# Another order of expert products around layer 1's projections, and the first row maxima transposed in the ring before the attention

## What is computed

```python
def reference(x, ...):
    x = x + _L0_conv_ref(_gn(x), ...)          # 6 heads of 16, bias from rel_pos_h and rel_pos_w
    t = _to_tokens(x)
    t = t + _L1_attn_ref(_ln_t(t), ...)        # causal, 6 heads of 16
    t = t + _L1_ffn_ref(_ln_t(t), ...)         # all experts computed, weighted by masked gates
    return _from_tokens(t, x)
def _L1_ffn_ref(x, ...):
    h = jax.nn.gelu(jnp.einsum('bsd,edh->ebsh', x, w1) + b1[:, None, None, :], approximate=False)
    y = jnp.einsum('ebsh,ehd->ebsd', h, w2) + b2[:, None, None, :]
    return jnp.einsum('bse,ebsd->bsd', masked, y)
```

## Time and profile before

| | us |
|---|---|
| median of 3 runs | 2209.66 |
| lowest and highest run | 2201.82 to 2210.24 |
| the profiled execution | 2204.84 |
| its span, first to last instruction | 2203.0 |
| PE busy | 1855.9 (84%) |
| DVE busy | 1255.3 (57%) |
| ACT busy | 1121.6 (51%) |
| mean granted TensorE clock | 0.933 of full speed |

### The profile page before, as it was taken

One profiled execution on the slowest core, in us unless ns is written; L12 is line 12 of the kernel. 1 busy time (PEld: TensorE's weight loads), 2 busy tenths in 40 slices (PEclk: granted clock), 3 DMA queues, 4 the chain that ended last, 5 costly groups with the idle time before them and its releaser, 6 DMA issues.

```text
span 2203.0 us, 28891 instructions
## 1 busy us (share of the span) xinstructions
PE 1855.9 (84%) x9314; PEld 743.8 (34%) x9408; DVE 1255.3 (57%) x2512; ACT 1121.6 (51%) x1423; POOL 141.7 (6%) x68
## 2 busy tenths in 40 slices
PE   0279568998899988998889988999889988999848
PEld 0123223343333432343333433344323433334324
DVE  5384367736665566736675466645676456744611
ACT  0326434675456734566446734567346744555423
POOL 0000000200020000200011000200002000200020
PEclk9669769999999999999999999999899999999979
DMA  1702530263004430163002530063202530002100
GB/s 44 134 10 53 91 72 21 50 97 65 21 18 92 57 77 11 47 110 65 22 18 56 89 80 11 18 115 64 42 22 49 96 65 13 18 10 54 28 10 7
DMA packets 55741, 111.43 MB, mean 51 GB/s; under 512 B 17687, under 2 KB 18904, under 8 KB 54041
## 3 DMA queue, kind: packets, MB, share of 16 engines
q1 hardware_dynamic: 54040, 109.06, 26.3%
q10 hardware_dynamic: 1536, 0.30, 0.1%
HBM read 61.82 MB, written 34.60 MB: 44 GB/s over the span
## 4 chain that ended last, share of the span: by engine, by line
PE 67%; DVE 18%; issue 4%; ACT 4%; DMA 4%; SPq 1%; POOL 0%; DVEq 0%; POOLq 0%; ACTq 0%
PE psOM L629 15%; PE psS L574 12%; PE psT L607 8%; PE psT L606 7%; PE psT L741 6%; DVE mx L1236 6%; PE psS L755 4%; PE psT L609 3%; PE psT L536 3%; DVE mrow L1338 2%; DVE x L1347 2%; DVE qb L1365 1%; DMA qr<-negb 1%; PE psOM L561 1%; PE psT L545 1%
## 5 line engine op out<-in xcount | busy, mean ns | idle before, releaser
L968 ACT ACTIVATE probs<-psT 128x1024 f32<-128x1024 f32 (+7 forms) x768 | 622.6, 837 | 535.2 <-PE psT L607 265.9
L1236 DVE TENSOR_REDUCE mx<-psS 128x1 f32<-128x512 f32 (+3 forms) x1152 | 704.2, 643 | 305.2 <-PE psS L574 225.1
L607 PE MATMUL psT<-qb,kb 97*128 97x512 f32 x768 | 416.1, 586 | 6.9 <-DMA qb<-negr 5.9
L629 PE MATMUL psOM<-probs,v 128*32 128x512 f32 (+3 forms) x2688 | 386.2, 560 | 22.6 <-ACT probs L968 12.0
L574 PE MATMUL psS<-ka,qa 128*128 128x512 bf16 x722 | 283.4, 401 | 22.1 <-DVE mx L1236 14.0
L606 PE MATMUL psT<-qa,ka 128*128 128x512 bf16 x720 | 278.2, 386 | 11.4 <-DVE resid L1225 4.0
L741 PE MATMUL psT<-xf,w1s 97*128 97x512 f32 x384 | 193.8, 633 | 4.2 <-ACT probs L1025 2.4
L1365 DVE TENSOR_TENSOR qb<-psOM,qa 32x768 fp32r<-32x768 f32 x128 | 121.8, 952 | 127.7 <-ACT qa L1008 126.0
L609 PE MATMUL psT<-qr,kr 97*128 97x512 bf16 (+3 forms) x576 | 185.6, 349 | 5.3 <-DMA qr<-negb 1.6
L755 PE MATMUL psS<-probs,w2s 128*96 128x512 f32 x384 | 187.9, 612 | 0.0
L574 PEld LDWEIGHTS psS<-ka,qa 128*128 128x128 bf16 x768 | 71.6, 98 | 301.3 <-DVE mx L1236 265.1
(11 more groups left out here) (143 smaller groups left out, 1598.8 us busy)
## 6 DMA issues: line engine op xcount, KB each, us to landing
scr<-split SPq DMA_DIRECT2D x32, 576.0 KB, 4.3
scr<-qb SPq DMA_DIRECT2D x16, 768.0 KB, 6.7
qr<-scr SPq DMA_DIRECT2D x48, 192.0 KB, 6.8
au<-ot SPq DMA_DIRECT2D x192, 32.0 KB, 2.0
lb<-ot SPq DMA_DIRECT2D x192, 32.0 KB, 2.0
qr<-scr SPq DMA_DIRECT2D x48, 128.0 KB, 4.3
kr<-scr SPq DMA_DIRECT2D x48, 128.0 KB, 7.3
qa<-scr SPq DMA_DIRECT2D x32, 128.0 KB, 3.8
```

Source lines behind the costliest of these rows:

```text
L607: last = mm(o[:, a:b], kb[:, h, ks], qb[:, h, a:b], start=False, stop=True)
L629: last = mm(psO[j:j + 2 * HD, a - c * HALF:HALF], v[:, kt, 2 * p + hh, :], probs[:, (2 * kt + hh) % 4, a:(c + 1) * HALF], start=kt == 0, s ...
L968: A(probs[:, n % 4, q0:T], psT[:, t_slot(ts, m), q0:T], ACT.Exp).then_inc(t_free, 1)
L1236: V.reduce_max(mx[layer][:, p % 2, (h % 2) * NT + t, kc:kc + 1], psS[:, s_bank(st, fill), 0:max_cols(layer, t, kc)], AX).then_inc(s_free, 1)
```

## The change

The list MIX is reordered between `u3` and `m0`, `lev` goes ahead of `V0`, `u10` ahead of `b1`, and a step `tmax` is added at its end. `tmax` transposes the first maxima into a slot of psT instead of psM (`first_rows`), and ACT negates them and issues the DMA there (`first_negated`). `attention(it, 1)` no longer begins with the transposition, and the wait for the additions goes to the first value product. The counts of the semaphores follow. The number of instructions is the same but for the loop's waits.

```diff
-MIX = seq("gate gates u0 u1 R0 d0 H0 L0 H1 L1 v0 u2 d1 v1 ln den R1 u3 H2 L2 d2 H3 u4 res d3 nrm L3 u5 d4 tr u6 R2 H4 L4 d5 q0 q1 V0 lev V1 "
-          "H5 L5 u7 d6 u8 R3 H6 L6 d7 H7 L7 u9 b0 d8 b1 u10 m0 m1 m2 m3 d9 m4 m5 m6 "
-          "u11 m7 m8 m9 m10 d10 m11 m12 b2 m13 m14 d11 m15 b3")
+MIX = seq("gate gates u0 u1 R0 d0 H0 L0 H1 L1 v0 u2 d1 v1 ln den R1 u3 d2 u4 H2 L2 u5 res H3 d3 nrm L3 u6 d4 d5 tr R2 H4 L4 q0 q1 lev V0 d6 V1 "
+          "u7 H5 L5 R3 u8 d7 H6 L6 H7 L7 u9 b0 d8 u10 b1 m0 m1 m2 m3 d9 m4 m5 m6 "
+          "u11 m7 m8 m9 m10 d10 m11 m12 b2 m13 m14 d11 m15 b3 tmax")
...
             def transpose_max(it, layer, p):
                 ms, n = att_m(layer, p)
-                if layer == 1 and p == 0:
-                    pe.wait_ge(t_free, upto("t_free", it, ms, 0))
-                else:
-                    pe.wait_ge(rowmax, upto("rowmax", it, ms, p if layer else n + 1))
+                pe.wait_ge(rowmax, upto("rowmax", it, ms, n + 1))
...
                     if kt == 0:
+                        if layer == 1 and p == 0:
+                            pe.wait_ge(y_free, upto("y_free", it, st, 0))
                         pe.wait_ge(o_free, upto("o_free", it, st, p))
...
                 if layer == 1:
-                    pe.wait_ge(y_free, upto("y_free", it, st, 0))
-                    transpose_max(it, 1, 0)
                     pe.wait_ge(l1_in, upto("l1_in", it, "attn1", 0))
...
+            def first_rows(it, st):
+
+                fs = fills(st, kind_of(it))
+                reduced = len([f for f in fs[:fs.index(("max", 2 * NT - 1)) + 1] if not by_act(f)])
+                pe.wait_ge(t_free, upto("t_free", it, st, reduced))
+                o = take_mixed(it, st, ("tmax", 0))
+                mm(o[0:2 * NT, 0:P], mrow[:, 0, :], ident, is_transpose=True, start=True, stop=True).then_inc(t_full, 1)
...
+            def first_negated(it, st):
+
+                fs = fills(st, kind_of(it))
+                fill = fs.index(("tmax", 0))
+                act.wait_ge(t_full, upto("t_full", it, st, fill + 1))
+                act.wait_ge(negmax_in, upto("negmax_in", it, st, 0))
+                A(negm[1][:, 0, :], psT[0:2 * NT, t_slot(st, fill), 0:P], ACT.Copy, scale=-1.0).then_inc(ta_free, 1)
+                act.wait_ge(ta_free, upto("ta_free", it, st, len([f for f in fs[:fill + 1] if by_act(f)])))
+                act.dma_start(qr[C:C + 1, 0:2, :].rearrange("o h (t q) -> o (h t) q", q=P),
+                              negm[1][:, 0, :]).then_inc(negmax_in, 16)
...
                 if layer == 1:
-                    neg_max(it, 1, 0)
                     exp_table()
```

More of the change, by code:

```diff
@@ L110, in fills @@
 def fills(stage, kind):
-    return [x for x in steps(stage, kind) if x[0] in ("up", "max", "res", "tr", "qk", "val", "val0")]
+    return [x for x in steps(stage, kind) if x[0] in ("up", "max", "tmax", "res", "tr", "qk", "val", "val0")]
 def by_act(what):
-    return what[0] in ("up", "tr", "val", "val0")
+    return what[0] in ("up", "tr", "tmax", "val", "val0")
 _ATT = {"attn0": 1, "attn1": 1}
@@ L134 @@
     "t_full": {"p_qkv0": 4, "attn1": ATT_FILLS, "attn0": QKV_AT, "qkv0": 2,
-               "attn0b": ATT_FILLS - QKV_AT, "rel": 2, "a": NE * HJ, "next_mix": 6 + 2 * NT},
+               "attn0b": ATT_FILLS - QKV_AT, "rel": 2, "a": NE * HJ, "next_mix": 7 + 2 * NT},
     "s_full": {**{s: len(m) for s, m in MAX_STEPS.items()}, "norm": 4, "a": 2 * NE},
-    "m_full": {"attn1": PAIRS, "lead": 1, "attn0": PAIRS - 1, "a": 1},
+    "m_full": {"attn1": PAIRS - 1, "lead": 1, "attn0": PAIRS - 1, "a": 1},
     "gsum_full": _GN, "gsum_free": _GN,
@@ L148 @@
     "rowmax": {"attn1": PAIRS - 1, "lead": 1, "attn0": PAIRS - 1},
-    "negmax_in": {"attn1": 16 * PAIRS, "lead": 16, "attn0": 16 * (PAIRS - 1)},
+    "negmax_in": {"attn1": 16 * (PAIRS - 1), "lead": 16, "attn0": 16 * (PAIRS - 1), "next_mix": 16},
     "p_used": {s: ATT_FILLS for s in _ATT},
@@ L159 @@
     INCS[f"{_r}_free"] = dict(INCS[f"{_r}_full"])
-INCS["ta_free"] = {"p_qkv0": 2, "rel": 2, "a": NE * HJ, "next_mix": 3}
+INCS["ta_free"] = {"p_qkv0": 2, "rel": 2, "a": NE * HJ, "next_mix": 4}
 INCS["r_free"] = {"qkv0": 2}
@@ L214, in att_m @@
 def att_m(layer, p):
-    return ("attn1", p) if layer else ("attn0", p - 1) if p else ("lead", 0)
+    return ("attn1", p - 1) if layer else ("attn0", p - 1) if p else ("lead", 0)
 def next_layer0(it):
@@ L663, in attention @@
                     else:
-                        pe.wait_ge(negmax_in, upto("negmax_in", it, st, 16 * (p + 1)))
+                        pe.wait_ge(negmax_in, upto("negmax_in", it, st, 16 * p))
                     for kt in range(NT):
@@ L826, in mix @@
                         first_maxima(it, "mix", n)
+                    elif what == "tmax":
+                        first_rows(it, "mix")
+            def first_rows(it, st):
[4 more added lines that the diff above has]
+                mm(o[0:2 * NT, 0:P], mrow[:, 0, :], ident, is_transpose=True, start=True, stop=True).then_inc(t_full, 1)
             def group_means(it, st):
@@ L937, in neg_max @@
                 act.wait_ge(m_full, upto("m_full", it, ms, n + 1))
-                act.wait_ge(negmax_in, upto("negmax_in", it, ms, 16 * max(p - 1, 0) if layer else 0))
+                act.wait_ge(negmax_in, upto("negmax_in", it, ms, 16 * max(p - 2, 0) if layer else 0))
                 A(negm[layer][:, p % 2, :], psM[0:2 * NT, 0:P], ACT.Copy, scale=-1.0).then_inc(m_free, 1)
@@ L1044, in mix @@
                         rel_high(it, "mix", n)
+                    elif what == "tmax":
+                        first_negated(it, "mix")
                     elif what == "up":
@@ L1239, in maxima @@
                         dve.wait_ge(s_free, upto("s_free", it, st, fill + 1))
-                        dve.wait_ge(m_full, upto("m_full", it, st, max(p - 1, 0)))
+                        dve.wait_ge(m_full, upto("m_full", it, st, max(p - 1 - layer, 0)))
                         V.tensor_tensor(mrow[:, p % 2, :], mx[layer][:, p % 2, :, 0], mx[layer][:, p % 2, :, 1],
```

## The result

The changed kernel took 2224.82 us (median of 6 runs, 2217.95 to 2227.11), the kernel before 2205.89 us beside it (median of 6 runs, 2201.82 to 2210.24): 1.008 times as long, 95% interval 1.0061 to 1.0099. It is slower by 0.8%, and 2228 us was forecast. The page of its profiled execution (2224.82 us), to be held against the earlier trace rows: the span and the granted clock in 40 slices.

A forecast was written before the change was run, and what follows sets the result against it. The mix was taken as bound by a chain of hand-overs, so by queue order: 21.6 - 2.3 - 9.9 + 9.9 - 2.0 + 3.6 = +20.9 us on 2204.8 us, named 2228 us, range 2207 to 2246 us.

The forecast's parts named there:

- Up to u7: Mix from gate to u7: norm and tr 1.35 us late, d6 fills 1.7 us, u7 at 515.4 against 515.47.
- From u7 to b0: Rounds 0 to 5: R3 waits for L5 behind u7's Gelu, PE idle 3.95 us, b0 3.25 us later.
- rival 4: R3 does not wait for L5; six rounds gain 1.7 us each instead of losing 3.6; 2187 us, chance 0.06.
- From b0 on: Mix after b0: u10 saves PE 0.4 us, second addition delays first maxima; whole reorder taken as 3.6 us per round.
- The clock: Half clock at V1 goes in three mixes, -9.9 us; new half clock behind R3 in six rounds, +9.9 us.
- Rival 1: The stall ahead of R3 stands, but the clock does not fall there; 9.9 us less, 2218 us, chance 0.2.
- Rival 2: Half clock lasts longer (d7, u9, first maxima), or falls around the projections stay; 2240 us, chance 0.17.
- The written-out seams: Behind rounds 0, 5 and 6: two products lie ready when DVE ends its additions; 0.65 us each, -2.0 us.
- The jumps back: Four loop jumps: PE's restart counts from its branch, 0.9 us later each; +3.6 us, bounds -1.2 and +3.6.
- The level: Whole kernel: half of the 4.9 us between profiled execution and median added, 2225.7 us becoming 2228 us.
- Rival 3: The clock stays up at the seven seams, -24.5 us; with the clock of Rival 1 2193 us, chance 0.07.

The follow-up runs named there:

- e3: The changed kernel with H5 and L5 ahead of u7, and u8 ahead of R3; 2175.26 us, ratio 0.9872 to the kernel before.
- e7: The changed kernel with only u8 moved ahead of R3, H5 still behind u7's Gelu; 2198.22 us, ratio 0.9969 to the kernel before.
- e8: The changed kernel with only H5 and L5 moved ahead of u7, u8 still behind R3; 2198.20 us, ratio 0.9982 to the kernel before.
- e4: The changed kernel with two unused copies of u8's products between u7 and R3; 2224.82 us, ratio 1.0085 to the kernel before.
- e1: The changed kernel with the old order of steps, keeping only the new transposition tmax; 2203.92 us, ratio 0.9988 to the kernel before.
- e5: The changed kernel with twelve unused transpositions ahead of the real one in tmax's slot; 2214.87 us, ratio 1.0056 to the kernel before.
- e12: A searched new order of the same steps (2161.69 us) with twelve unused transpositions added at its end; 2153.06 us, ratio 0.9760 to the kernel before.

## Why the prediction was right, and where it was off

**Up to u7.** Right in every step. The walk had `tr` 32.05 us behind the gate, q0 35.5, V0 39.85, u7 43.55; round 3 of the changed kernel shows 32.1, 35.4, 39.75 and 43.3. d6 stands between the values without a wait.

**From u7 to b0.** Right. 3.95 us of idle ahead of R3 were forecast, 3.90 us are there, and the releaser is DVE's L5. With the half clock b0 was to come 58.5 + 1.65 = 60.15 us behind the gate; it comes at 60.1 us in rounds 2 to 5, and at 61.7 and 62.1 us in rounds 1 and 0, where a fall of the clock just behind the gate delays all. Runs e3, e7 and e8 show the two mechanisms apart, and rival 4, by which R3 does not wait for L5, is out.

**From b0 on.** The sum is near (+2.1 and +2.8), but not by its reason. In four of the six rounds b0 to b3 is 22.9 us, as before: u10 ahead of b1 costs nothing. The 2.8 us are two rounds (24.6 and 24.4 us) with a new fall of the clock there. The late additions that I charged with 0.35 us are covered.

**The clock.** Both terms were right in place and sign. No fall is left at V1 (there were three, 3.3 us each), and behind R3 there is one in all six rounds. In rounds with nothing else disturbed it costs 1.8 us; I had taken 1.65. Rival 1 is refuted in all six rounds. Rival 2 is only half so: the falls at the projections did not stay, but two came later, in rounds 2 and 4. That the idle PE ahead of R3 lets the clock fall, and work there keeps it up, is shown by e4, which fills the hole. The Trainium skill (TensorE: Matmul & The Clock Gate, What's actually happening) says that the throttled state is the default and that activity releases it. The traces agree: e4's clock stays at 1.00 where PE is busy, and falls at the next wait.

**The written-out seams.** Right in what they are, a little small: -0.85, -1.0 and -0.8 us where I had -0.65 each. DVE's first maximum stands directly behind its last addition. I counted only DVE's 0.77 us of waiting; the products that lie ready also shorten what follows.

**The jumps back: the mis-sized term.** I let the restart count from PE's branch and charged +3.6 us. It measured +0.4 us, inside the bounds of -1.2 and +3.6 us. The reading was right, and the fetch that the prediction names for it is there as well: the branch's own record fills the wait, and a packet of instructions lands within it at every jump. Two sizes in it were wrong. The branch moved by 1.55 us and not by 1.0, because in the kernel before it began at 0.11 to 0.30 us behind b3's start and not at b3's end. And the term took the length of the jump to be the same in both kernels, without a reason: it was 4.76 us on average before and 3.72 us after, since three of the four jumps had two packets before and none had after. So the branch ended 0.51 us later; 0.41 us of that came back behind it, where the transposition no longer stands, and 0.1 us per jump is left. The shorter jumps are luck as far as the runs tell: nothing in the prediction foresaw them, and e1 and e4, with the same code at the jump, had some of the long ones. With 0.4 us in place of 3.6 the sum would be 17.7 us; that the forecast's 20.9 us is so near to 20.0 is owed in part to the other rows of the table, whose misses add up to +2.3 us.

**The level.** Half of the 4.9 us between profile and median was added. With six runs the median of the kernel before is 2205.9 us, 1.1 us above its profiled execution, so 2.5 us of the 3.2 us between 2228 and 2224.8 us are this addition.

**Rival 3.** The clock did fall behind all seven seams, so it did not come about here. But e5 and e12 show that its mechanism exists: with 1.47 us of unused transpositions at each seam the kernels were 8.6 to 10 us faster.

## What to carry to other kernels

An order that fills a hole on one engine must be walked on all of them: here d6 filled 1.7 us ahead of u7, and the Gelu that moved ahead of H5 cost 3.9 us of idle two steps later. Ahead of each instruction that waits, ask what stands in its releaser's queue without need (H5 behind u7's Gelu), and what stands behind the waiting one that could go ahead (u8); each was worth 26.6 us here. Such a walk with the durations of one trace gave this kernel to 0.3 us within a mix and found one 2.5% faster than before, while differences of under 10 us over the whole kernel can come from where the clock falls and from how long the jumps last. And where an idle time ends with "issue" behind a jump, look up the record of the branch itself before giving it a cause.
